# Attention between two expert layers: the transfer of the row maxima is issued by ScalarE instead of the sync engine

## What is computed

```
x = x + 0.5 * ffn(layernorm(x))                       # top-2 of 8 experts, and a shared expert
x = x + attention(layernorm(x))
x = x + 0.5 * ffn(layernorm(x))

q, k, v = proj(Wq), proj(Wk), proj(Wv)
scores = (q . k  +  q . rel_emb[clip(i - j, -128, 128) + 128]) / sqrt(8)
attn = softmax(scores)                                # over keys
combined = gate * (attn . v) + (1 - gate) * global_attn(elu(q) + 1)
out = combined @ Wo.T + bo
```

## Time and profile before

| | us |
|---|---|
| median of 3 runs | 2693.93 (2687.33 to 2699.09) |
| profiled execution, its own time | 2715.97 |
| span of the profiled execution, first to last instruction | 2712.9 |
| TensorE (PE) busy | 2113.0 (78%) |
| VectorE (DVE) busy | 1521.1 (56%) |
| ScalarE (ACT) busy | 1389.6 (51%) |
| GpSimd (POOL) busy | 1129.5 (42%) |

### The profile page before, as it was taken

One profiled execution on the slowest core, in us unless ns is written; L12 is line 12 of the kernel. 1 busy time (PEld: TensorE's weight loads), 2 busy tenths in 40 slices (PEclk: granted clock), 3 DMA queues, 4 the chain that ended last, 5 costly groups with the idle time before them and its releaser, 6 DMA issues. The chain is left out here.

```text
span 2712.9 us, 48244 instructions
## 1 busy us (share of the span) xinstructions
PE 2113.0 (78%) x15592; PEld 1461.1 (54%) x15592; DVE 1521.1 (56%) x4202; ACT 1389.6 (51%) x2765; POOL 1129.5 (42%) x1594
## 2 busy tenths in 40 slices
PE   5656897721899999999998999999998665699650
PEld 4444675510456666556665656666665544567440
DVE  7554564533556666666665666666664655455441
ACT  4444664410566566665665656666663444466430
POOL 1655003465444444444434443444431355300556
PEclk9777998855799999999999999999998877899885
DMA  5244886622788777878878877888782114488662
GB/s 139 93 139 164 233 240 188 198 75 47 221 237 234 221 221 222 232 223 221 225 211 221 224 206 213 234 223 229 216 228 61 38 39 135 144 240 237 195 178 75
DMA packets 382766, 496.50 MB, mean 183 GB/s; under 512 B 43956, under 2 KB 316212, under 8 KB 382516
## 3 DMA queue, kind: packets, MB, share of 16 engines
q1 hardware_dynamic: 326644, 308.21, 43.3%
q0 software_dynamic: 53248, 184.07, 20.6%
q10 hardware_dynamic: 2624, 1.13, 0.2%
HBM read 252.56 MB, written 214.95 MB: 172 GB/s over the span
## 5 line engine op out<-in xcount | busy, mean ns | idle before, releaser
L1311 DVE CUSTOM_DVE_ANT_0 at_junk<-at_ps_s,at_rel 128x512 bf16<-128x512 f32 x1024 | 666.4, 689 | 416.6 <-PE at_ps_s L953 399.8
L1090 ACT ACTIVATE at_probs<-at_ps_t 128x512 f32<-128x512 f32 x1024 | 558.9, 595 | 518.8 <-PE at_ps_t L938 518.2
L938 PE MATMUL at_ps_t<-tab_ident,at_rel 128*128 128x128 f32 x3328 | 497.9, 290 | 0.0
L517 POOL DMA_INDIRECT ffn_zg<-rows_z,rows_home x256 | 248.8, 972 | 481.9 <-issue 400.5
L938 PEld LDWEIGHTS at_ps_t<-tab_ident,at_rel 128*128 128x128 f32 x3328 | 373.5, 146 | 82.3 <-issue 23.5
L718 DVE TENSOR_TENSOR ffn_h<-ffn_silu,ffn_ps_gate 128x512 f32<-128x512 f32 x248 | 170.4, 687 | 352.5 <-ACT ffn_silu L480 279.1
L507 POOL DMA_INDIRECT rows_x<-ffn_xe,rows_index x256 | 254.4, 994 | 264.4 <-ACT ffn_xe L459 187.2
L925 PE MATMUL at_ps_t<-at_qs,at_ks 25*128 25x256 f32 x2048 | 301.2, 336 | 74.1 <-DMA at_qs<-at_mrow 73.9
L925 PEld LDWEIGHTS at_ps_t<-at_qs,at_ks 25*128 25x128 f32 x2048 | 189.9, 189 | 299.9 <-ACT at_probs L1090 135.0
L480 ACT ACTIVATE ffn_silu<-ffn_ps_mid 128x512 f32<-128x512 f32 x248 | 148.8, 600 | 390.1 <-PE ffn_ps_gate L319 196.8
L978 PE MATMUL at_ps_v<-at_probs,at_v 128*32 128x256 f32 x4096 | 336.7, 401 | 0.2 <-ACT at_probs L1090 0.2
(11 more groups left out here) (196 smaller groups left out, 3365.7 us busy)
## 6 DMA issues: line engine op xcount, KB each, us to landing
at_band<-at_src POOLq DMA_DIRECT2D x256, 574.0 KB, 4.9
at_rel<-at_band SPq DMA_DIRECT2D x512, 143.5 KB, 3.8
ffn_w_expert<-rows_w SPq DMA_DIRECT2D x92, 768.0 KB
ffn_xg<-rows_x SPq DMA_DIRECT2D x92, 256.0 KB
rows_z<-ffn_y SPq DMA_DIRECT2D x92, 256.0 KB
rows_x<-ffn_zero SPq DMA_DIRECT2D x46, 256.0 KB
at_rel<-at_band SPq DMA_DIRECT2D x64, 128.0 KB, 3.5
at_rel<-at_band SPq DMA_DIRECT2D x64, 127.5 KB, 3.0
```

Of the source, the lines that this page charges most:

```text
L517: pool.indirect_dma_start(zg[:, t % RZ, k, s, :], None, rows.z[g], bass.IndirectOffsetOnAxis(home[:, q, k, t % PAIR * T + s, :], 0)).then_ ...
L938: ins = pe.matmul(ps_t[:, i, HALF * n + P * l:HALF * n + P * (l + 1)], rel[:, c % RREL, l, 2 * hp + i, kb * P:(kb + 1) * P], ident[:], sta ...
L1090: act.activation(probs[:, kp, 2 * hp + i].rearrange("p n q -> p (n q)"), ps_t[:, i, :], ACT.Exp).then_inc(exp_done.sem, 1)
L1311: dve.tensor_tensor_reduce(out=junk[:, i, :], in0=ps_s[:, i, :], in1=rel[:, c % RREL, l, h, :], scale=1.0, scalar=-3e38, op0=ALU.add, op1= ...
```

## The change

The function `maxima_in` moves, word for word but for the engine, from the sync engine's program to ScalarE's. SP issued it in slot `c` for item `c + 1` behind the first four `fetch_rel`; ScalarE issues it in slot `c` for item `c + 1` at the start of the fourth step, ahead of that step's two exponentials. The semaphores, the source, the destination and the size stay as they are.

```
--- before.py
+++ after.py
@@ ScalarE @@
+            def maxima_in(c):
+
+                j = c
+                act.wait_ge(m_row.sem, m_row.at(j, 1))
+                m_ring, n = pair_ring(m_in, c)
+                at = (ROW * R2 + par_of(c)) * SETS * S + set_of(c) * S + HALF * half_of(c)
+                to = bass.AP(qs[:].tensor, at, [[32 * R2 * SETS * S, HG], [1, HALF]])
+                act.dma_start(to.bitcast(F32), mrow[:, c % R2, :].bitcast(F32)).then_inc(m_ring.sem, 16)
...
             def slot(c):
                 for k in range(4):
+                    if k == 3 and item(c + 1) is not None:
+                        maxima_in(c + 1)
                     if item(c) is not None:
                         exponent(c, k)
@@ sync @@
-            def maxima_in(c):
...
             def slot(c):
                 if item(c + 3) is not None:
                     fetch_rel(c + 3, 0)
-                if item(c + 1) is not None:
-                    maxima_in(c + 1)
                 if coming(c) is not None:
                     stack(c, 0)
```

## The result

The changed kernel takes 2804.33 us (median of 4 runs, 2790.42 to 2819.03) against 2696.51 us before (2687.33 to 2701.68): the ratio is 1.0384 [1.0347, 1.0421], slower by 108 us. The prediction was 2664. The profiled execution took 2819.03 us with a span of 2816.5, 103.6 more than before.

The account below looks back on a forecast made before the run. PE was taken to bound the attention. Slots other than 4 gave -9 us, slot 4 -13 and the clock -8, together -30 us off the median of 2693.9: 2664 us, range 2630 to 2702.

Parts of the forecast that it names:

- ACT's part at nothing: ScalarE's 128 added issues cost nothing, covered by the step-2 copy and PE's turn; uncovered they would cost 70 us.
- The landing, "I take 2.7, the middle": The maxima transfer on ScalarE's queue lands 2.7 us after issue, between bounds of 2.2 and 3.3 us.
- The upper bound, 3.3: Longest landing allowed: a transfer without a stall, issued on SP at 1300.39, was in place by 1303.66.
- The time left in each slot: From step 2's last work to the next L925: 3.25, 2.84 or 2.45 us by slot, 1.71 in slot 4.
- Slot 4: Stall at L925 shrinks from 3.46 to about 1.1 us, mostly lost again at L963; net -13 us.
- the third rival: The gain is masked: landing in 2.95 us, the queries bound slot 4, 2689 us, no measurable change; chance 0.26.
- The clock: Of 40 us lost in PE's half-level clock stretches over the attention, a fifth is regained: -8 us, from 0 to -20.
- the -8 of the sum: The clock's term in the forecast sum, for PE's half-level stretches in the attention: -8 us.
- The slow rival: Maxima issued into the band write, landing in 3.3 us or more: 2722 us, or 2767 at 3.7; chance 0.11.
- its point of decision: The maxima landing from which the slower case decides: 3.05 us.

Follow-up runs that it names:

- act_step2: The changed kernel with ScalarE issuing the maxima one step earlier, at the slot's third step: 2487.96 us, ratio 0.9833 to the kernel before.
- sp_late: The kernel before with SP's issue of the maxima moved behind the slot's second four band transfers: 2710.09 us, ratio 1.0716 to the kernel before.
- small reads: The kernel before with each shifted-band transfer reading 32 columns instead of 256 to 287, from item 4 on: 2668.58 us, ratio 0.9887 to before.
- the repeat: Both kernels run again unchanged on one chip: before 2530.96 us, changed kernel 2656.06 us, ratio 1.0487.

## Why the prediction was wrong

- **ACT's part at nothing: right** (ratio 1.0006). Its queue runs further ahead than I said: it issues 0.35 us ahead of the step-2 copy (0.7 where an odd job follows it), not 0.1 behind its start.
- **The landing, "I take 2.7, the middle": the step that failed.** It is 4.56 us at the median. The upper bound, 3.3, was made from a transfer that had been issued away from a band write: the one at 1300.39 was issued 3.9 us behind one and 0.13 ahead of the next, and by the semaphore's last update it landed in 2.3 us. I had set the one that took 6.4 us aside as a matter of SP's queue, though it was issued right behind a band write, as each would be on ScalarE. I had the row that said so too, the band write at 1309.70 with the copy at 1310.54, and weighed it as "speaks for the high end" of a range in which it was not contained.
- **The time left in each slot: right, but for slot 4.** Put the measured median landings of slots 0 to 7 (4.5, 3.6, 4.7, 5.6, 4.65, 4.7, 4.9 and 3.55 us), less ACT's head start (0.35, in slots 2 and 5 0.7), against the times of the prediction: slot 0 lands in 4.5, less 0.35, less 2.45 is 1.7 us, and the measured stalls sum to 25.0 for 16 slots. In the same way slot 3 gives 38 us (measured 35.8), slot 5 18 (19.6), slot 2 11 (12.0), slot 6 33 (27.6) and slot 7 12 (12.7). With slot 4's 39 (29.8) and slot 1's none (4.3) the sum is 178 us, and 166.8 were measured. In slot 4 the time left is 2.5 us now, not 1.71, which gives the 29.8. So of the terms of the stalls the landing was the wrong one.
- **Slot 4: the sign was right.** Its stalls fell from 46.5 to 29.8 us, though its transfer too lands in 4.65. L963's wait there is gone rather than grown (the 12.0 us of its row stand ahead of the first item), because L925 still waits past the queries' arrival; in act_step2, where it does not, L963 waits 48.8 us in all, 36.8 of them in slot 4, which is the masking of the third rival.
- **The clock: wrong in sign**, +18.5 us of busy time against the -8 of the sum. Stretches at the half level (1.2 instead of 2.4 GHz) went from 20 to 35 in the attention, 102 to 154 us. Such a stretch lies behind the stall of 1393.21 shown above; after's windows, in the columns of the earlier trace rows, with the clock and the share of the transfer engines third and second from the end:

```profile
1393.00:1397.00 4.00, 3.79 (x25) 2.47 (x27) 2.28 (x7) 1.56 (x3) 1.30 (x2) 0.58 0.85 246
1397.00:1400.00 3.00, 3.00 (x31) 2.04 (x28) 2.40 (x7) 1.58 (x4) 0.42 (x2) 0.99 0.43 124
```

  More stalls come with more of them: act_step2, with 1.2 us of waits for the maxima, has 12, and sp_late, with 207.2, has 46. I had counted on fewer stalls.
- **The slow rival, at 0.11, was what happened**, with the cause it names and its point of decision passed; at 3.8 us with the 0.1 it gave 2767. What should have raised its chance is the table above: sorting the 128 landings of before by the distance to the last band write. The rule of the Trainium skill that the prediction cites with it ("DMA: Bandwidth & Descriptors", section "Issuing engines are not separate DMA queues") is borne out: 5.05 us on SP's queue, 4.61 on ScalarE's. The other one, of the same page's "Queues, rings and completion order", that engines serve the rings in turn, was not a promise that the neighbours' traffic hardly counts: 1.63 us became 3.8 beside a band write, on a queue with short transfers alone.

What stays open is how the band write holds the small transfer up. In the median slot its first packet moves 2.5 us after the issue, against 1.2 when nothing is near, so 1.3 of the 3.0 us of delay lie ahead of its first byte. No run tells whether that is in making the write's descriptors or at the transfer engines.

## What to carry to other kernels

When a small transfer is moved, sort all its landings in the old trace by what else was in flight at the issue, and take the price from those that match the new place, not from the median or the nearest slot. A queue of its own does not protect it: here one step's difference on the same queue made 0.983 out of 1.04 to 1.05. And when a late transfer is brought forward, ask what is next on the same queue; bringing the queries forward as well made the band's reads late and gained nothing.

## What the runs showed of the hardware

- A 4 KB transfer within the core's memory lands 1.6 us after its issue when little is under way (94 transfers on SP's queue with small reads; on ScalarE's only the last three of after, 1.62), and in 4.6 to 5.0 us when it is issued within 2 us behind a 574 KB write to DRAM.
- Issuing a transfer on ScalarE (0.54 us) 128 times more left the time as it was: ratio 1.0006 [0.9978, 1.0033].
- The same kernel took 2533 and 2536 us on two chips and 2693 on a third; in the first comparison, whose chip is not on record, it took 2697. The attention has little part in that: from the first to the last issue of the maxima it took 1363.9 us in the first comparison and 1349.2 in the repeat, and after took 1469.0 and 1471.7. The difference lies in the layers around it (the first issue of before comes at 703.1 us and at 621.3). The ratio of the change is 1.0384 there and 1.0487 in the repeat, so a ratio does not carry over exactly either.
